# Layer 2's stages of values, each issued as two halves of 256 tokens in a kernel with a planned order

## What is computed

```python
x = x + attn_a(layernorm(x), ...)   # layer 1: 16 heads, keys of 8 + 32 columns
x = x + ffn(layernorm(x), ...)      # top-1 of 8 experts, 128 -> 512 -> 128
x = x + attn_b(layernorm(x), ...)   # layer 2: differential attention
x = x + ffn(layernorm(x), ...)

# attn_b, after the rotary turn; 16 heads, two score maps each
attn1 = einsum('bhid,bhjd->bhij', q1, k1) * scale
attn2 = einsum('bhid,bhjd->bhij', q2, k2) * scale
probs = softmax(attn1) - lam * softmax(attn2)
out = einsum('bhij,bhjd->bhid', probs, v)      # v has 16 columns a head
```

## Time and profile before

| | before |
|---|---|
| median of 3 runs | 1642.0 us (1638.96 to 1644.62) |
| profiled execution | 1644.09 us, span from the first to the last instruction 1642.4 us |
| busy, share of the span | PE 87%, DVE 72%, ACT 66%, POOL 44% |
| mean granted clock of PE | 0.964 of full speed |

### The profile page before, as it was taken

How to read it: one execution, slowest core, us unless ns; L and a number is a source line. 1 busy time by engine, 2 the same in 40 slices (tenths; PEclk the granted TensorE clock), 3 DMA queues, 4 the chain that set the end, 5 groups by cost and what they waited for, 6 DMA issues and landing times.

```text
span 1642.4 us, 27700 instructions
## 1 busy us (share of the span) xinstructions
PE 1430.6 (87%) x9478; PEld 626.9 (38%) x9528; DVE 1189.8 (72%) x2067; ACT 1080.1 (66%) x1811; POOL 729.7 (44%) x794
## 2 busy tenths in 40 slices
PE   4599999999999998889888888899899887999846
PEld 2223333335653332355532223244344322545236
DVE  4477778777768878756786788977688889667424
ACT  2166666676556776676677777777687877777712
POOL 5310244334424663477856533354754600656213
PEclk9799999999999999899999999999999999999959
DMA  6745444775733343876312120551320204542022
GB/s 176 240 113 139 121 134 136 223 230 151 249 115 79 96 139 113 247 230 183 114 35 59 33 65 20 188 167 59 107 70 21 72 21 137 170 125 92 1 97 80
DMA packets 127281, 199.06 MB, mean 121 GB/s; under 512 B 16967, under 2 KB 94564, under 8 KB 127142
## 3 DMA queue, kind: packets, MB, share of 16 engines
q1 hardware_dynamic: 120182, 184.32, 37.9%
q0 software_dynamic: 6240, 12.71, 2.3%
q10 hardware_dynamic: 720, 0.26, 0.1%
HBM read 125.65 MB, written 73.46 MB: 121 GB/s over the span
## 4 chain that ended last, share of the span: by engine, by line
PE 66%; DVE 11%; ACT 6%; DMA 5%; issue 5%; POOL 3%; SPq 2%; another core or an unknown queue 0%; ACTq 0%; POOLq 0%; DVEq 0%
PE ps L1133 19%; PE ps L1099 12%; PE ps L1120 11%; DVE Mb L1461 7%; PE ps L1217 5%; ACT P L1309 5%; PE ps L1230 5%; PE ps L1067 4%; PE ps L1141 2%; PE ps L1228 1%; POOL ROW L1375 1%; DMA X<-xs 1%; PE ps L1167 1%; PE ps L1083 1%; PE ps L1186 1%
## 5 line engine op out<-in xcount | busy, mean ns | idle before, releaser
L1461 DVE TENSOR_REDUCE Mb<-ps 128x2 f32<-128x1024 f32 (+1 forms) x955 | 940.8, 1011 | 326.7 <-PE ps L1099 308.8
L1309 ACT ACTIVATE P<-ps 128x1024 f32<-128x1024 f32 (+1 forms) x1065 | 807.0, 787 | 341.8 <-PE ps L1120 329.8
L1120 PE MATMUL ps<-STK 32*128 32x512 f16 (+1 forms) x1536 | 414.5, 388 | 63.5 <-ACT P L1309 27.7
L1099 PE MATMUL ps<-STK 32*128 32x512 f16 (+1 forms) x1536 | 405.2, 387 | 45.0 <-DVE Mb L1461 16.1
L1133 PE MATMUL ps<-P,V 128*32 128x512 f32 x3072 | 417.2, 616 | 8.1 <-ACT P L1309 6.1
L1099 PEld LDWEIGHTS ps<-STK 32*128 32x128 f16 (+1 forms) x1536 | 101.6, 93 | 302.2 <-issue 102.9
L1120 PEld LDWEIGHTS ps<-STK 32*128 32x128 f16 (+1 forms) x1536 | 104.8, 93 | 273.5 <-ACT P L1309 85.0
L1729 POOL DMA_INDIRECT xs<-ROW,slot x64 | 63.7, 996 | 122.9 <-DVE slot L1551 107.8
L1736 POOL TENSOR_TENSOR TH<-TH,Z 128x512 f32<-128x512 f32 x65 | 82.6, 1272 | 74.4 <-ACT Z L1355 73.4
L1217 PE MATMUL ps<-XT,WE 128*128 128x128 f32 x752 | 99.9, 276 | 9.2 <-issue 5.5
L1133 PEld LDWEIGHTS ps<-P,V 128*32 128x32 f32 x3072 | 60.7, 108 | 121.1 <-issue 98.2
(11 more groups left out here) (169 smaller groups left out, 1502.3 us busy)
## 6 DMA issues: line engine op xcount, KB each, us to landing
WE<-in_we SPq DMA_DIRECT2D x94, 576.0 KB
STK<-qka SPq DMA_DIRECT2D x64, 480.0 KB
qka<-HL SPq DMA_DIRECT2D x96, 256.0 KB
STK<-qkb SPq DMA_DIRECT2D x64, 256.0 KB
qkb<-HL SPq DMA_DIRECT2D x96, 128.0 KB
X<-xs SPq DMA_DIRECT2D x84, 129.5 KB
xs<-pad SPq DMA_DIRECT2D x8, 1036.0 KB, 7.6
qka<-HL SPq DMA_DIRECT2D x48, 128.0 KB
```

The costliest lines, as they stand in the source:

```text
L1099: mm = eng.matmul(ps[:, bank + i, :], l_, r_, start=True, stop=True)
L1120: mm = eng.matmul(ps[:, bank + i, :], l_, r_, start=True, stop=True)
L1309: eng.activation(P[:, st % 3, j:j + n, :], ps[:, bank:bank + n, :], ACT.Exp, scale=SCALE_A if g < 4 * B else SCALE_B).then_inc(sem("exp"), 1)
L1461: eng.tensor_reduce(Mb[:, g % 2, at:at + 4 * n - 3:4], ps[:, bank:bank + n, :], AX, ALU.max).then_inc(sem("mx"), 1)
```

## The change

In layer 2 (`g >= 4 * B`) a stage of values is issued as two: `pv_half` with query tokens 0 to 255 and `pv` with 256 to 511, each of four products of 256 columns. The planner knows them as two stages of 0.57 instead of one of 1.02, asks for the second once the first is placed, and may place other work between. Only the second half raises the semaphore on which P's and the bank's next users wait. At `kt == 0` the first half carries the start flag, the second doesn't. Layer 1 keeps its whole stages.

```diff
--- before.py
+++ after.py
@@ -159,7 +159,7 @@
 
 
 STAGES = {
-    "smax": ("tensor", 0.216), "score": ("tensor", 0.216), "pv": ("tensor", 1.02), "mrow": ("tensor", 0.11), "oturn": ("tensor", 0.45),
+    "smax": ("tensor", 0.216), "score": ("tensor", 0.216), "pv": ("tensor", 1.02), "pv_half": ("tensor", 0.57), "mrow": ("tensor", 0.11), "oturn": ("tensor", 0.45),
     "hturn": ("tensor", 0.45), "feat": ("tensor", 0.86), "vproj": ("tensor", 1.0), "aturn": ("tensor", 0.45), "oproj": ("tensor", 1.3), "gturn": ("tensor", 0.45), "glogit": ("tensor", 0.8),
     "gplace": ("tensor", 0.5), "xturn": ("tensor", 0.11), "up": ("tensor", 1.1), "down": ("tensor", 1.1),
     "rowmax": ("vector", 1.13), "normal": ("vector", 0.6), "join": ("gpsimd", 0.8), "split": ("gpsimd", 1.6), "ln_stats": ("vector", 1.3),
@@ -180,7 +180,7 @@
          "weights_p": 3.0, "scatter": 4.0, "fill": 5.0, "send": 4.0}
 FROM = [(19.77, 0.27), (32.89, 0.43), (59.5, 0.9), (83.5, 0.55), (100.00, 0.10)]
 
-MAIN = ("smax", "rowmax", "score", "expo", "pv")
+MAIN = ("smax", "rowmax", "score", "expo", "pv", "pv_half")
 ENGINES = ("tensor", "vector", "scalar", "gpsimd", "sync")
 
 
@@ -305,7 +305,9 @@
             if kt == 0 and g:
                 yield from after(("ocopy", (g - 1,)))
             yield from after(("exped", (g, kt)))
-            yield from do(st / 4 + 0.85, "pv", g, kt)
+            if g >= 4 * B:
+                yield from do(st / 4 + 0.85, "pv_half", g, kt)
+            yield from do(st / 4 + 0.85, "pv", g, kt, us=0.57 if g >= 4 * B else 1.02)
 
     def maxima_back():
         for g in range(NG):
@@ -1120,7 +1122,8 @@
                     mm = eng.matmul(ps[:, bank + i, :], l_, r_, start=True, stop=True)
                 mm.then_inc(sem("st"), 1)
 
-            def pv(g, kt):
+            def values(g, kt, lo, hi):
+
                 b, hh = batch_of(g), g % 4
                 vw = 16 if b < B else 20
                 if kt == 0:
@@ -1130,9 +1133,16 @@
                 on.wait_ge("exp", scored_step[g, kt])
                 for j in range(4):
                     h = 4 * hh + j
-                    mm = eng.matmul(ps[32 * j:32 * j + 32, OB, :], V[:, b % 3, kt, vw * h:vw * h + 32], P[:, st % 3, j, :],
-                                    start=(kt == 0), stop=(kt == 3))
-                mm.then_inc(sem("pv"), 1)
+                    mm = eng.matmul(ps[32 * j:32 * j + 32, OB, lo:hi], V[:, b % 3, kt, vw * h:vw * h + 32], P[:, st % 3, j, lo:hi],
+                                    start=(kt == 0 and lo == 0), stop=(kt == 3), skip_group_check=True)
+                return mm
+
+            def pv_half(g, kt):
+                values(g, kt, 0, 256)
+
+            def pv(g, kt):
+
+                values(g, kt, 256 if g >= 4 * B else 0, 512).then_inc(sem("pv"), 1)
 
             def oturn(g):
                 bank = bank_for("oturn", g)
@@ -1232,7 +1242,7 @@
                 mm.then_inc(sem("fo"), 1)
 
             stages = dict(hturn=hturn, feat=feat, vproj=vproj, smax=smax, mrow=mrow, score=score,
-                          pv=pv, oturn=oturn, aturn=aturn, oproj=oproj, gturn=gturn, glogit=glogit, gplace=gplace, xturn=xturn, up=up,
+                          pv=pv, pv_half=pv_half, oturn=oturn, aturn=aturn, oproj=oproj, gturn=gturn, glogit=glogit, gplace=gplace, xturn=xturn, up=up,
                           down=down)
             for stage, index in order["tensor"]:
                 stages[stage](*index)
```

## The result

The changed kernel takes 1670.5 us (median of 4 runs, 1667.7 to 1676.5) against 1643.3 us before (4 runs): 1.0167 times, with a 95% interval of 1.0121 to 1.0213. It is slower by 27 us where 6 to 7 us of gain were forecast, and beyond the range (1617 to 1662).

The account below looks back on a forecast made before the run. Layer 2 was taken as a loop of three engines waiting by turns, PE nearest full. On the chain, 51 us of PE cost (terms 1 and 2) against 56 us of gain (term 3) gave 1636 us, range 1617 to 1662.

Parts of the forecast that it names:

- term 3: Layer 2: scores come 0.43 us earlier at a stage's middle, 157 of 473 DVE and ACT waits shrink: -67 us.
- term 2: Layer 2 on PE: scores cut into shorter stretches pack worse on the array's rows, 125 more slots: +27 us.
- With nothing between, about nothing: On PE: a stage issued as two halves with nothing between them costs about nothing more.
- Term 1: Layer 2 on PE: each of 243 split stages costs 0.23 us more, less 6 us for fewer other changes: +50 us.
- the clock stays at 0.98: PE's granted clock in layer 2, 0.98 before, got no term; each hundredth named as about 8 us of PE.
- PE becomes the bound: Layer 2: mode changes and worse packing paid in full, decided in windows from 1200 us on; 1663 us, chance 0.30.

Follow-up runs that it names:

- e2: The changed kernel's order on every engine, but whole stages of values issued where the second halves stood, nothing at the first: 1626.7 us, ratio 0.9878 to before.
- e14: As e2, whole stages at the second half's place, but planned with 0.63 us for a half instead of 0.57: 1607.9 us, ratio 0.9877 to before.
- e10: The changed kernel's order, both halves issued side by side where the second half stood: 1635.9 us, ratio 0.9967 to before.
- last step of the decomposition: From e10 to the changed kernel, same order: the first half goes to its own, earlier place; costs 2.0%, 33 us.
- e12: Halves only in the 36 groups of layer 2 with few experts, whole stages in the others, planned anew: 1666.6 us, ratio 1.0189 to before.
- e4: Halves only in the 28 groups of layer 2 with many experts, whole stages in the others, planned anew: 1645.5 us, ratio 1.0022 to before.
- e13: e4's order, with whole stages issued where the second halves stood: 1626.2 us, ratio 0.9986 to before.
- e6: The changed kernel's order, whole stages issued where the first halves stood, nothing at the second: 1661.1 us, ratio 1.0146 to before.
- e7: The kernel before with whole stages, only the planner told a layer 2 values stage takes 1.14 us instead of 1.02: 1659.9 us, ratio 1.0154.
- e15: Before's own order, on PE alone each layer 2 values stage moved behind the next two rows of scores if these follow at once: 1698.8 us, ratio 1.0447.

## Why the prediction was wrong

**The order's gain (term 3 less term 2)** was right in its sign and too large. On the chain it was 56 less 18 (27 x 0.66), 38 us; e2 has it alone, 20 us (1.2%), and e14 the same. Term 3 took a third of all waits as standing beside values and let each shrink by 0.43 us. In e2 the waits fell by 12 us, in e14 by 38. Of term 2 nothing shows there: e2's work on PE at full clock is an estimated 822 us, before 823.

**"With nothing between, about nothing"** was right for the stage (1003 ns against 998) and wrong for the kernel: side by side costs 0.9% in the new order and 1.0% in the old one.

**Term 1** priced a single split rightly: 0.57 and 0.32 us in the trace. The sum made of it did not come out. Terms 1 and 2 put 77 us on PE; at full clock its work grew by some 33 (823 to 856; e2 822, e10 831). That the busy time rose by 74 is luck: 40 of these are half clock. In groups 64 to 79, at full clock, a quarter of term 1's 33 us on the chain (50 at 66%) would be 8, and the table has 1.3 against e2. The 33 us of the last step of the decomposition have the size of term 1 by chance too: the step also moves a half, and its clock falls by 0.018.

**The step that failed for good is that the clock stays at 0.98.** The sum has it at nothing. The text named it as what would spoil the forecast and even had a price, about 8 us of PE for a hundredth in the window, but no rival, no chance and no term; at that price the 0.94 that came is some 32 us. In 39 executions of the kernel before in the three sessions up to e12 time and clock go together (correlation -0.87): 1634.0 us at 0.972, 1649.0 at 0.952, and by a straight line 10.8 us for each 0.01. The fourth session alone gives 10.1, e4's and e13's ten executions 10.9 and 9.3, e10's 13.9. 0.01 of 1640 us is 33 us at half clock, so such time costs a third of itself. By that line the changed kernel's 0.936 against 0.963 is 29 us, all of its loss; at equal clock it would stand at some 1641 us, where the sum of the forecast's terms (-5) comes near enough, with costs and gains that are both too large. This is a relation between runs, and the clock was never changed by itself. The traces bear it out: the loss lies in the groups in which the clock was down, and the half at 1386.77 takes 1.01 us in place of 0.57.

What keeps the clock down is not shown. In one order it was 0.957 whole, 0.954 side by side (the two overlap: 0.953 to 0.970 and 0.949 to 0.962) and 0.936 with the first half at its own place. But it was 0.943 with whole stages at the earlier place (e6), and 0.947 and 0.930 with whole stages in other orders (e7, e15). So it goes with the order too and doesn't need the changes of mode.

Of these changes themselves: the Trainium skill, "TensorEngine Tiling (Array Packing)", Tiling Modes, says that a change of tiling mode drains TensorE. The trace agrees, with 0.10 us on the way in and 0.14 on the way out (0.57 less 0.43 of streaming).

**The rival "PE becomes the bound"** (0.30) had the side and nearly the size, 1663 us. It said that this is decided where PE is fullest, from 1200 us on. There it is the other way round: the changed kernel gains 11 us on before in groups 64 to 79, at full clock, and by e4 and e12 halves in the groups with many experts cost 0.2% all told, in those with few 1.9%. The rival had the time, and not the cause.

**Open:** why parts side by side cost 1% when a stage takes 5 ns more, of which the clock is 7 of 17 us by the line; what keeps the clock down once it has fallen; and whether the 33 us of the last step come from the changes of mode or from the first half's earlier place. By the line above 20 of them (0.018) go with the clock and 13 don't. Each new plan also moves the time by itself (e7: +1.5%), so e4 and e12, which are plans of their own, are weaker evidence than e2, e10 and the changed kernel, which share one.

## What to carry to other kernels

Splitting a block so that others can pass may be worth more as a way to plan than as a way to run: take the order that the finer pieces give, and issue the block whole at the later place (e2, e14: 1.2% faster, where the split itself is 1.7% slower). It has to be tried: e13, made the same way for 28 groups, gained nothing. Test an order and the instructions that fill it apart, with the same order in both, and ask of each step whether it also moves something. And give the granted clock a term of its own with a price from the runs (here 11 us for 0.01) wherever a change gives PE a new order; a range that leaves it out is too narrow. Before a rise in busy time counts as work, take out what was done at half clock.

## What the runs showed of the hardware

- At half clock a half stage with its exit takes 1.01 us against 0.57, 1.8 times.
- Products of zeros over a quarter of the array's columns went with a granted clock as high as products over all of them (0.9575 and 0.955, from 0.936), and the added 31 us on PE cost nothing that the runs could tell (ratios 1.0140 and 1.0156, changed kernel 1.0167).
- In the changed kernel's layer 2 the clock fell behind stretches of 10 us in which PE was busy 64 to 84%, with no idle piece over 2.6 us, and then stayed down for 7 to 31 us while PE was busy 73 to 100%. What decides how long was not found.
- Within one kernel, run to run, the granted clock varies from 0.952 to 0.972, and the time goes with it, by 15 us between these two.
